# Preparing a sequence in another order: projections, row transfers and the norm reciprocal ahead of the pair loop

## What is computed

```
xp, z  = x @ Wx.T, x @ Wz.T
Bm, Cm = rmsnorm(x @ WB.T) * w + bias, rmsnorm(x @ WC.T) * w + bias   # 64 heads x 128
dt, lam, theta = softplus(x @ Wdt.T), sigmoid(x @ Wlam.T), x @ Wth.T
Bm, Cm = rope(Bm, cumsum(theta * dt)), rope(Cm, cumsum(theta * dt))
h_t = alpha_t h_(t-1) + beta_t B_(t-1) x_(t-1) + gamma_t B_t x_t ;  y_t = C_t h_t
out = (y * silu(z)) @ Wout.T
```

## Time and profile before

| what | value |
|---|---|
| median of 3 runs | 3788.26 us (3786.51 to 3813.47) |
| the profiled execution | 3786.05 us, of which the span of the trace is 3784.2 us |
| mean granted TensorE clock | 0.904 of 2.4 GHz |
| busy share | PE 88%, DVE 76%, ACT 47%, POOL 46% |
| reciprocal L1105 of pairs 0 and 1, sequences 0 to 3 | at 631.3, 1340.1, 2045.6, 2687.5 us |
| first `F_dve1`, sequences 0 to 3 | at 645.0, 1349.5, 2055.9, 2697.3 us |

### The profile page before, as it was taken

One profiled execution on the slowest core, in us unless ns is written; L12 is line 12 of the kernel. 1 busy time (PEld: TensorE's weight loads), 2 busy tenths in 40 slices (PEclk: granted clock), 3 DMA queues, 4 the chain that ended last, 5 costly groups with the idle time before them and its releaser, 6 DMA issues.

```text
span 3784.2 us, 84141 instructions
## 1 busy us (share of the span) xinstructions
PE 3313.2 (88%) x26980; PEld 2650.1 (70%) x26980; DVE 2880.4 (76%) x4774; ACT 1790.7 (47%) x3552; POOL 1733.4 (46%) x1420
## 2 busy tenths in 40 slices
PE   5299986899998889999867999998899998799990
PEld 4288874777776667777755788775577876688880
DVE  5265654999999489999845999994799999465663
ACT  1144434556564256555415666651566665144440
POOL 3433321555555145666501666662366665132326
PEclk7699998999998799999868999997999999699995
DMA  9898974564644154555204555541455453388883
GB/s 389 292 301 278 292 229 141 156 191 153 195 151 136 49 171 142 163 152 160 83 8 128 166 156 162 162 120 55 138 162 150 154 164 111 143 283 295 282 283 120
DMA packets 343082, 668.79 MB, mean 177 GB/s; under 512 B 62272, under 2 KB 183232, under 8 KB 341824
## 3 DMA queue, kind: packets, MB, share of 16 engines
q1 hardware_dynamic: 318272, 598.73, 49.6%
q0 software_dynamic: 24576, 67.14, 6.0%
HBM read 484.03 MB, written 180.62 MB: 176 GB/s over the span
## 4 chain that ended last, share of the span: by engine, by line
PE 57%; DVE 16%; issue 9%; DMA 7%; SPq 6%; ACT 2%; POOL 1%; DVEq 1%; POOLq 0%; ACTq 0%
PE bank L59 14%; PE bank L496 9%; PE bank L509 6%; PE bank L1245 5%; PE bank L1206 4%; PE bank L1275 4%; DVE xbc L1134 3%; SPq L738 3%; PE bank L487 3%; PE bank L1076 3%; DVE tmp L1158 2%; PE bank L1214 2%; PE bank L1266 2%; DMA rr_bc<-rr_dram 2%; DVE xc L1140 2%
## 5 line engine op out<-in xcount | busy, mean ns | idle before, releaser
L59 PE MATMUL bank<-xh,wb 128*128 128x512 f32 x2048 | 717.7, 432 | 36.9 <-DVE sqs L1095 25.0
L1084 ACT ACTIVATE xbc<-bank,norm_w 128x512 f32<-128x512 f32 x512 | 350.0, 684 | 610.5 <-PE bank L59 539.2
L1166 POOL TENSOR_TENSOR rot<-rot,tmp 128x512 f32<-128x512 f32 x256 | 332.2, 1297 | 608.0 <-DVE tmp L1158 608.0
L1158 DVE SCALAR_TENSOR_TENSOR tmp<-xbc,bias,cs_sn 128x1024 f32<-128x1024 f32 x256 | 450.2, 1758 | 0.0
L59 PEld LDWEIGHTS bank<-xh,wb 128*128 128x128 f32 x2048 | 364.0, 196 | 113.6 <-DVE sqs L1095 32.3
L1167 POOL TENSOR_TENSOR rot<-rot,tmp 128x512 f32<-128x512 f32 x256 | 440.9, 1722 | 0.0
L496 PE MATMUL bank<-wgu,xgT 128*128 x2048 | 424.2, 330 | 0.3
L59 PE MATMUL bank<-xl,wb 128*128 128x512 f32 x1024 | 419.5, 410 | 0.0
L556 DVE TENSOR_TENSOR hh<-sg,bank 128x96 f32<-128x96 f32 x512 | 130.2, 254 | 328.9 <-ACT sg L547 326.0
L1158 DVE SCALAR_TENSOR_TENSOR rot<-xbc,bias,cs_sn 128x1024 f32<-128x1024 f32 x256 | 377.0, 1473 | 0.1
L538 ACT ACTIVATE xgT<-bank 128x256 f32<-128x256 f32 x512 | 196.7, 384 | 377.3 <-PE bank L487 375.8
(11 more groups left out here) (210 smaller groups left out, 6735.0 us busy)
## 6 DMA issues: line engine op xcount, KB each, us to landing
wb<-watt_dram SPq DMA_DIRECT2D x96, 1024.0 KB, 6.4
yd<-ys SPq DMA_DIRECT2D x128, 512.0 KB, 4.4
rr_bc<-rr_dram SPq DMA_DIRECT2D x128, 512.0 KB, 6.4
wd<-w_down SPq DMA_DIRECT2D x512, 96.0 KB
xd<-xg SPq DMA_DIRECT2D x16, 2048.0 KB, 23.9
watt_dram<-wb SPq DMA_DIRECT2D x32, 1024.0 KB, 5.6
dt_bc<-row_dram SPq DMA_DIRECT2D x256, 128.0 KB, 5.4
al_bc<-row_dram SPq DMA_DIRECT2D x256, 128.0 KB, 2.9
```

What stands on the lines that cost most here:

```text
L59: ins = e.matmul(dst, a, m, start=start and c == 0, stop=stop and c == n - 1, skip_group_check=not (start and stop))
L1084: e.activation(xbc[j % 4][:, i, :], XBANK[i % 2][:, :], ACT.Copy, scale=norm_w[:, i:i + 1])
L1158: ins = e.scalar_tensor_tensor(o[:, 2 * ty:2 * ty + 2, :], X[:, i, :].unsqueeze(1).to_broadcast([P, 2, SEQ]), bias_of(i), cs_sn[j % 2][:, ...
L1166: e.tensor_tensor(R[:, 2 * ty, :], R[:, 2 * ty, :], tmp[:, 2 * ty + 1, :], ALU.subtract)
```

## The change

On PE the A parts 0 and 1 of pair 1 come directly after pair 0, then ss of pair 0, the other two parts, `inner(0)`, the `dect` transposes, ss of pair 1, `inner(1)`, and then `T_pe` of pair 0, which so far stood in `pairs_pe` behind `x1`; `inner(2)`, `inner(3)` and A of pair 2 come last. On ACT `R_act` moves into the preparation, ahead of the copy to `decay_t`, and A of pair 2 is cut in two and stands behind `T_act2` and `T_act3` of pair 0. On DVE the first `A_dve` of pair 1 moves ahead of the wait for alpha, the reciprocal `R_dve` into the middle of the `x1` products, and `A_dve` of pair 2 behind `T_dve2`. On SP `R_sp` is cut into three: its first DMA, the reciprocal's operand, is issued before the wait for the row stores, the other two between the broadcasts. The splits of sequence 0's weights for pairs 2 and 3 move along.

```diff
@@ -782,21 +782,25 @@
                                        start=k == 0, stop=k == KD - 1)
             ins.then_inc(e_p1.sem, 1)
             e.wait_ge(e_xl.sem, e_xl.at(KD * (b + 1)))
-            A_pe(e, b * NP, 0, None if is_first(b) else (b - 1) * (NP // 2) + 1)
+            first = None if is_first(b) else (b - 1) * (NP // 2) + 1
+            A_pe(e, b * NP, 0, first)
+            A_pe(e, b * NP + 1, 1, first, [0, 1])
+            ss_pe(e, b * NP, 0)
+            A_pe(e, b * NP + 1, 1, first, [2, 3])
             inner(0)
-            inner(1)
-            ss_pe(e, b * NP, 0)
-            A_pe(e, b * NP + 1, 1, None if is_first(b) else (b - 1) * (NP // 2) + 1)
-            e.wait_ge(e_pd.sem, e_pd.at(b * PREP_STEPS + 3))
-            inner(2)
-            inner(3)
-            ss_pe(e, b * NP + 1, 1)
             e.wait_ge(e_p4.sem, e_p4.at(b + 1))
             e.nop(nofuse=True)
             for k in range(NC):
                 ins = e.matmul(W[2][CL:P, k * CL:(k + 1) * CL], dect[:, k * CL:(k + 1) * CL], ident[0:NH, 0:NH],
                                start=True, stop=True)
             ins.then_inc(e_p5.sem, 1)
+            ss_pe(e, b * NP + 1, 1)
+            inner(1)
+            e.wait_ge(e_pd.sem, e_pd.at(b * PREP_STEPS + 3))
+            e.wait_ge(e_p3.sem, e_p3.at(2 * b + 2))
+            T_pe(e, b * NP, 0, first)
+            inner(2)
+            inner(3)
             A_pe(e, b * NP + 2, 2, None if is_first(b) else (b - 1) * (NP // 2) + 2)
 
         def prep_act(e, b):
@@ -829,9 +833,12 @@
             e.activation(alpha, dth, ACT.Exp, scale=neg_a[:, 0:1]).then_inc(e_pc.sem, 1)
             A_act(e, b * NP + 1, 1, [0, 1])
             A_act(e, b * NP + 1, 1, [2, 3])
+            R_act(e, b * (NP // 2))
             e.wait_ge(e_p5.sem, e_p5.at(b + 1))
             src = W[2][CL:P, :].rearrange("p (k a q) -> p k q a", k=NC, a=2)
             e.activation(decay_t[CL:P, :, :, :], src, ACT.Copy).then_inc(e_p3.sem, 1)
+            if is_first(b):
+                wb_high_act(e, 2, 0, 1)
 
         PREP_STEPS = 12
         e_pd, e_pu, e_p6 = ev("e_pd"), ev("e_pu"), ev("e_p6")
@@ -872,6 +879,7 @@
                 ins = e.scalar_tensor_tensor(dtk[:, s], steps_of(s), 0.0, tok(sp_l, s + 1), ALU.max, ALU.add)
             step(ins)
             A_dve(e, b * NP, [1])
+            A_dve(e, b * NP + 1, [0])
             e.wait_ge(e_pc.sem, e_pc.at(6 * b + 6))
             step(e.tensor_copy(alpha0, alpha))
             step(e.memset(starts(alpha0), 0.0))
@@ -883,7 +891,6 @@
             e.memset(end_rows[:, :, 0:1], 0.0)
             ends = dect.rearrange("p (k c) -> p k c", k=NC)[:, 0:NC - 1, CL - 1]
             e.tensor_copy(end_rows[:, :, 1:NC], ends.unsqueeze(1).to_broadcast([NH, 32, NC - 1])).then_inc(e_p4.sem, 1)
-            A_dve(e, b * NP + 1, [0])
             A_dve(e, b * NP + 1, [1])
             e.tensor_tensor(gam, lamk[:, 0], dtk[:, 0], ALU.mult)
             step(e.tensor_scalar(oml, lamk[:, 1], -1.0, 1.0, ALU.mult, ALU.add))
@@ -895,6 +902,10 @@
             assert n[0] == PREP_STEPS
             wide = lambda a, t: a[:, t, :].unsqueeze(2).to_broadcast([P, NH, HP])
             for t in range(TT):
+                if t == 2 and is_first(b):
+                    wb_low_dve(e, 2, 0)
+                if t == 2:
+                    R_dve(e, b * (NP // 2))
                 e.wait_ge(e_p2.sem, e_p2.at(TT * b + t + 1))
                 src = xbanks[t][:, :].rearrange("p (n d) -> p n d", n=NH)
                 ins = e.tensor_tensor(x1[:, :, t, :], src, wide(coef, t), ALU.mult)
@@ -996,12 +1007,17 @@
                     dst = row_dram[:, kp, SEQ + a * (SEQ // 2):SEQ + (a + 1) * (SEQ // 2)]
                     s4 = hrow[r, SEQ:2 * SEQ].rearrange("p (t k c) -> p t k c", t=TT, k=2)
                     e.dma_start(dst.rearrange("q (t c) -> q t c", t=TT), s4[:, :, kp, :]).then_inc(a_roww.sem, 16)
+            R_sp1(e, b * (NP // 2))
             e.wait_ge(a_roww.sem, a_roww.at(8 * (b + 1)))
             e.nop(nofuse=True)
-            for m in range(2):
-                dt_sp(e, m, m)
-                al_sp(e, m, m)
-                end_sp(e, m, m)
+            dt_sp(e, 0, 0)
+            al_sp(e, 0, 0)
+            R_sp2(e, b * (NP // 2), 0)
+            dt_sp(e, 1, 1)
+            R_sp3(e, b * (NP // 2), 0)
+            end_sp(e, 0, 0)
+            al_sp(e, 1, 1)
+            end_sp(e, 1, 1)
 
         def row_sp(e, dst, q, cols, sem):
             for a in range(2):
@@ -1106,15 +1122,19 @@
 
         e_rc = ev("e_rc")
 
-        def R_sp(e, gm, par, cnt):
+        def R_sp1(e, gm):
             e.wait_ge(e_sr.sem, e_sr.at(gm + 1))
             e.nop(nofuse=True)
             e.wait_ge(e_rc.sem, e_rc.at(gm))
             e.nop(nofuse=True)
             e.dma_start(rc_in[:, :], stdr.rearrange("r (c w) -> r c w", w=32)).then_inc(a_r1.sem, 16)
+
+        def R_sp2(e, gm, par):
             e.wait_ge(e_rc.sem, e_rc.at(gm + 1))
             e.nop(nofuse=True)
             e.dma_start(rr_dram[par].rearrange("r (c w) -> (r c) w", w=32), rc[:, :]).then_inc(a_r2.sem, 16)
+
+        def R_sp3(e, gm, par):
             e.wait_ge(a_r2.sem, a_r2.at(gm + 1))
             e.nop(nofuse=True)
             e.wait_ge(e_xcc.sem, e_xcc.at(2 * (gm - 1)))
@@ -1122,6 +1142,11 @@
             for a in range(2):
                 src = rr_dram[par].rearrange("(g a) t -> a g t", a=2)[a:a + 1]
                 e.dma_start(rr_bc[par][CL * a:CL * a + CL, :, :], src.to_broadcast([CL, 4, SEQ])).then_inc(a_rr[par].sem, 16)
+
+        def R_sp(e, gm, par):
+            R_sp1(e, gm)
+            R_sp2(e, gm, par)
+            R_sp3(e, gm, par)
 
         def F_dve1(e, n, j, cnt):
             e.wait_ge(e_X.sem, e_X.at(4 * (n + 1)))
@@ -1457,14 +1482,12 @@
                     e.nop(nofuse=True)
                     al_sp(e, q + 2, j + 2)
                 if RG:
-                    R_sp(e, gm + 1, (j // 2 + 1) % 2, b * NB + it + 1)
+                    R_sp(e, gm + 1, (j // 2 + 1) % 2)
 
         def pairs_pe(e, b):
             N, NB, G = b * NP, NP // UN, b * (NP // 2)
-            e.wait_ge(e_p3.sem, e_p3.at(2 * b + 2))
             e.wait_ge(e_x12.sem, e_x12.at(b + 1))
             e.wait_ge(e_z0.sem, e_z0.at(b + 1))
-            T_pe(e, N, 0, None if is_first(b) else (b - 1) * (NP // 2) + 1)
             turn_pe(e, b, 0, True, False)
             with e.Fori(1, NB - 1) as it:
                 turn_pe(e, b, it, False, False)
@@ -1481,18 +1504,15 @@
 
         def pairs_act(e, b):
             N, NB, G = b * NP, NP // UN, b * (NP // 2)
-            R_act(e, G)
-            if is_first(b):
-                wb_high_act(e, 2, 0, 1)
-            A_act(e, N + 2, 2)
-            if is_first(b):
-                wb_high_act(e, 3, 1, 1)
-            e.wait_ge(e_x12.sem, e_x12.at(b + 1))
-            XP_act(e, N, 0, 0)
             T_act2(e, N, 0)
+            A_act(e, N + 2, 2, [0, 1])
             T_act3(e, N, 0)
             if is_first(b):
                 th_high_act(e, 2, 0, 1)
+                wb_high_act(e, 3, 1, 1)
+            A_act(e, N + 2, 2, [2, 3])
+            e.wait_ge(e_x12.sem, e_x12.at(b + 1))
+            XP_act(e, N, 0, 0)
             turn_act(e, b, 0, True, False)
             with e.Fori(1, NB - 1) as it:
                 turn_act(e, b, it, False, False)
@@ -1516,16 +1536,13 @@
 
         def pairs_dve(e, b):
             N, NB, G = b * NP, NP // UN, b * (NP // 2)
-            if is_first(b):
-                wb_low_dve(e, 2, 0)
-            A_dve(e, N + 2, [0])
-            if is_first(b):
-                wb_low_dve(e, 3, 1)
-            R_dve(e, G)
             T_dve1(e, N, 0, G + 1)
             T_dve2(e, N, 0)
             if is_first(b):
                 th_low_dve(e, 2, 0)
+            A_dve(e, N + 2, [0])
+            if is_first(b):
+                wb_low_dve(e, 3, 1)
             turn_dve(e, b, 0, True, False)
             with e.Fori(1, NB - 1) as it:
                 turn_dve(e, b, it, False, False)
@@ -1537,7 +1554,6 @@
 
         def pairs_sp(e, b):
             N, NB, G = b * NP, NP // UN, b * (NP // 2)
-            R_sp(e, G, 0, b * NB + 1)
             e.wait_ge(e_th.sem, e_th.at(N + 1))
             e.nop(nofuse=True)
             th_load_sp(e, b, 2, 0)
```

## The result

| what | before | changed |
|---|---|---|
| median | 3793.2 us (4 runs) | 3757.2 us (4 runs, 3751.97 to 3768.14) |
| ratio of the two | | 0.990, 95% interval 0.9855 to 0.9945 |
| profiled execution, its span | 3786.05, 3784.2 us | 3757.49, 3755.7 us |
| busy us of PE, DVE, ACT, POOL | 3313.2, 2880.4, 1790.7, 1733.4 | 3298.7, 2877.2, 1790.6, 1731.0 |

The change is faster: in this first measurement by 1%, 36 us between the medians (interval 21 to 55), where 13 were forecast.

A forecast was written before the change was run, and what follows sets the result against it. Two chains of nearly equal length were taken to end at each sequence's first product with `rr_bc` (L1134). Gains 1.9 + 2.9 + 2.4 + 5.0 = 12.2 from 3786.05 gave 3773.8 to 3776.0, said as 3775, range 3759 to 3787.

The forecast's parts named there:

- the walk of sequence 1: Unit-by-unit count of PE, ACT, DVE and SP times up to the first product with `rr_bc`: gain 1.9 us.
- theta's raw weights: Sequence 0, pair 2: issued by SP after all broadcasts at 624.4, taken as 5.6, there at 630.0; sequence gain 5.0.
- theta's size: PE's theta product counted as twelve matmuls, 2.8 us; theta of pair 1, behind pair 2, was to end last.
- case at full clock: Sequence 1 with PE at full clock: ACT's side would be last, a gain of 3.3 instead of 1.9.
- The clock term: PE stands 2.3 in pair 2, then runs at 1.2 GHz: part 2 ends at 1339.8, theta of pair 1 at 1345.5.
- The table load: ACT's load for the root, 1.28, was taken as done while idle; behind the wait it costs +0.9 a chain, 4 in all.
- The head start passes in full: Rival: angle and fraction 7.1 earlier move each first product by that, 28 in all, 3759; chance 0.13.
- Slower by the detour: Rival: pair 2's A parts 2 and 3 and pair 1's theta hang on dt(0)'s arrival; 3791 with the median; chance 0.08.
- The same time: Rival: finish line moves, but first turns wait again for a later transfer or POOL, eating the lead: 3787; chance 0.11.
- The operand does not do what it says: Rival: `R_dve` waits amid `x1` longer than the queue gained; 8.7 idle in sequence 0, covered if operand lands before about 618.
- signs of being wrong: L1134 of sequence 1 moved over 4 or later; `dt_bc` wait above 1 us; second DMA wait; difference in loops or experts.
- signs of being right: `rc_in` before broadcasts; angle some 7 earlier; `rr_bc` landed early; DVE idle on PE's theta or ACT's squares; clock near 0.5.

The follow-up runs named there:

- again: The changed kernel once more, unchanged, with more rounds, against the kernel before: ratio 0.9946 (0.9924 to 0.9968), 21 us by the ratio.
- again2: The changed kernel once more, unchanged, on another chip, against the kernel before: ratio 0.9926 (0.9894 to 0.9958), 28 us.
- a2_around: From the changed kernel: ACT does pair 2's parts 0 and 1 before pair 0's angle, 2 and 3 before its absolute value; ratios to before 0.9912 and 0.9903.
- sp_only: From the kernel before: only SP's queue in the changed order, PE, ACT and DVE as before; ratio 0.9968 (0.9951 to 0.9985), 12 us.
- pair1_late: From the changed kernel: pair 1's projections and first DVE add back in their old places; ratio to the kernel before 0.9987 (0.997 to 1.0004).

## Why the prediction was wrong

**What held.** The path was the right one up to the last chain, and the walk of sequence 1 held to 0.9 us up to the last square. As offsets, counted and then measured: pair 1's last matmul 26.4, 26.7; first row store 28.1, 27.9; `decay_t` copied 32.3, 32.9; reciprocal 34.2, 34.5; angle of pair 0 40.3, 39.4; square of part 1 of pair 2 45.1, 44.4; last square 50.4, 49.6. ACT's list was counted at 8 with no hole and took 8.2. In sequence 0 the reciprocal was counted to hold DVE for 8.7 under cover and held it for 8.59, and theta's raw weights were last, as the rows show (DVE, sequence 0, start 564.30; against the earlier trace rows):

```profile
611.63 0.35 DVE L1121 RECIPROCAL rc<-rc_in 128x32 f32<-128x32 f32 x1 [8.59 <-DMA rc_in<-decay_t]
...
615.53 0.70 DVE L1049 SCALAR_TENSOR_TENSOR bank<-bank,dt_bc 128x512 f32<-128x512 f32 x1 [1.83 <-DMA dt_bc<-row_dram]
...
627.12 0.42 DVE L971 TENSOR_TENSOR th<-th_raw,th 128x256 fp32r<-128x256 f32 x1 [8.18 <-ACT th L967]
...
635.59 2.33 DVE L1159 TENSOR_TENSOR xbc<-xbc,rr_bc 128x1024 f32<-128x1024 f32 x2
```

**The step that failed: theta's size.** "the theta product (twelve matmuls, 2.8)". It has six: the PE rows above go from 1310.96 to `inner(2)` at 1312.46, 1.5. The trace of the kernel before had it too, with theta of pair 1 as six matmuls from 1344.05 to 1346.74, 2.7 at the lower clock:

```profile
1344.05 1.19 PE L59 MATMUL bank<-xh,th 128*128 128x512 f32 x2 [6.12 <-DVE nfr L1042]
1345.04 0.63 PE L59 MATMUL bank<-xl,th 128*128 128x512 f32 x1
1345.46 1.06 PE L59 MATMUL bank<-xh,th 128*128 128x512 f32 x2
1346.32 0.63 PE L59 MATMUL bank<-xl,th 128*128 128x512 f32 x1
1346.74 1.06 PE L59 MATMUL bank<-xh,wb 128*128 128x512 f32 x2
```

I had taken the two parts of the weight split and the two halves of the contraction for four times three. This enters twice. Ahead of `inner(2)` it makes the angle 0.9 earlier than counted. And behind pair 2 it had put PE last: theta of pair 1 was to end at offset 52.4, and ended at 48.2, 1.4 before ACT's last square. So the wrong size also named the wrong last wait for sequences 1 to 3: it was ACT's list, which the prediction had only as its case at full clock.

**The clock term went with it.** I took 1.2 GHz behind the gap PE makes in pair 2, and charged 1.4 us a sequence. The gap came nearly as counted (2.3), 2.46 in sequence 1 (PE rows above) and 2.47 in sequences 2 and 3. Its effect did not: in sequence 1 the next pair of matmuls took 0.73, full clock, in sequence 2 it took 1.22, the lower level. The two PE rows of sequence 2:

```profile
2009.26 0.71 PE L59 MATMUL bank<-xh,th 128*128 128x512 f32 x2 [1.24 <-ACT decay_t L839]
...
2019.60 1.22 PE L59 MATMUL bank<-xh,wb 128*128 128x512 f32 x2 [2.47 <-ACT sqt L1103]
```

Yet from the angle to the product it took 12.7 in sequence 1 and 12.8 in 2 and 3: with six matmuls PE's theta is through before ACT's last square even where the lower clock came, in sequence 2 at 2025.5 against 2025.8. The Trainium skill (TensorE: Matmul & The Clock Gate, section "Why this matters for your kernels") advises against idle gaps of PE between bursts of matmuls, and means longer ones than this. The trace shows that the lower clock can follow here too, in two sequences of three, and that it costs nothing where PE is not last. In sequence 0 PE is last: theta of pair 1 took 2.6 at the lower clock, and DVE waited 0.66 for it.

**The sum with the right size.** With six matmuls and nothing else changed, the angle of sequence 1 starts 0.9 earlier, theta of pair 1, at half of the 3.1 counted for twelve, ends at 1343.1, and ACT's side, now last, comes 0.9 earlier than the 1344.2 + 1.95 of the prediction, to 1345.25: a gain of 4.2 where 1.9 was forecast and 4.3 measured. (With all six at the lower clock, 2.7 as in the rows above, it would be 3.3.) The same 2.3 more make 5.2 and 4.7 in sequences 2 and 3 (5.6 and 4.3 measured). In sequence 0 theta of pair 1 took 2.6 where I had 3.7, and the raw weights 4.7 from issue to use where I had 5.6: 7.0 instead of 5.0 (7.1 measured). Together 21.1, against 21.3 measured. So the forecast of 12.2 was short by 9, some 8 of it through the miscounted product and 0.9 through the raw weights.

In sequences 2 and 3 the agreement is partly luck. Their row stores moved by 4.5 and 3.8 us, where those of sequence 1 moved by 2.9 (from offsets 32.1, 31.8 and 30.8 to 27.6, 28.0 and 27.9), and the table load below took about as much back; the sum counts neither.

With 21 instead of 12 the forecast would have been 3766, inside the range. The other 9 us down to 3757.2 are not the mechanism's; they are taken up under "The rest of the 36 us".

**The table load.** I kept 1.3 in the range for a load behind the wait. It depends on the sequence. In the written-out sequence 1 ACT loads at 1306.05 and then waits 2.23 for the sums (rows above); in the loop body of sequences 2 and 3 it waits first:

```profile
2006.41 1.28 ACT L1116 ACT_TABLE_LOAD   x1 [3.60 <-PE bank L1092]
```

There theta of pair 0 waits 1.24 for `decay_t` (PE, 2009.26), and the angle starts at 40.3 and 40.9 instead of 39.4. From the first row store to the angle it took 12.7 and 12.9 there, against 11.5 in sequence 1; again and again2 show the same difference, 1.1 to 1.6.

**The rivals.** *The head start passes in full* (28 us, 3759): by the first total the nearest, by mechanism wrong. The angle came 8.0 earlier in sequence 1, and the first product 4.3: ACT's list took the rest, as a2_around shows by giving 3.7 of it back. a2_around itself comes near this rival, with 34 and 37 us. *Slower by the detour*: dt(0) was waited for only in sequence 0, 1.83. *The same time*: the changed kernel keeps its lead, sp_only 12 us of 19.5. *The operand does not do what it says*: true in a milder form, it does nothing. Of the prediction's own signs of being wrong two came: L1134 of sequence 1 moved by 4.3, over 4, and sequence 0 waited 1.83 for `dt_bc`, over 1. Of its signs of being right, the clock near 0.5 did not come in sequence 1, where the 3.3 us behind the gap have 1.00; in sequence 2 the 3.4 us behind it have 0.53. Its seven broadcasts behind `rr_bc` are six in the rows of SP, which changes nothing in the sum.

**The rest of the 36 us.** The first measurement is of four runs a side. The median before was 3788.26 when the forecast was made and 3793.2 with a fourth run, so 5 of the 36 lie on that side. Of the 28.5 between the two spans, 2.3 lie ahead of the first preparation, 21.3 in the offsets, 4.9 in the loops and the last expert phase. The stretch ahead of the first preparation holds no changed instruction; it took 566.6 and 576.9 in two executions before, 564.3, 578.7 and 568.5 after. The one from the fourth first product to the end took 1086.9 and 1093.0 before, 1089.2, 1088.0 and 1077.3 after. So single executions differ by 10 us and more in code that is the same, and a median of four carries it. The 4.9 did not come again either: all that lies outside the four offsets took 3532.7 and 3545.3 before, 3525.5, 3549.7 and 3546.5 after, on average 3539 and 3541. The three intervals of the changed kernel overlap from 0.9924 to 0.9945, 21 to 29 us, with the head start of 23 inside. So nothing here points to a gain in the loops; one of some 5 us is below what five profiles can tell, and it stays open.

## What to carry to other kernels

Find the instruction at which the steady loop starts and count every chain that ends there; when one is shortened, the next one's length decides, here ACT's, with two projections that had been moved behind the angle and its table load. Count matmuls of a helper in the trace, not in the code. A single wait or DMA that is moved earlier is worth nothing if the instruction behind it waits for something else, and parts of a reordering may only pay together: SP's order alone gave 19.5 of 23 us of head start, the whole change without pair 1's new place gave 9.

## What was not expected of the hardware

The same gap of PE, 2.46 to 2.47 us, was followed by 2.4 GHz in sequence 1 (the next pair of matmuls took 0.73) and by 1.2 GHz in sequences 2 and 3 (1.20 to 1.22), in all three profiles of the changed kernel. In pair1_late a gap of 2.46 to 2.51 was followed by 0.73 in all three sequences. So the length of the gap alone does not tell which level follows; no run here shows what does. And ACT's table load of 1.28 us stood ahead of a wait in the written-out code and behind the same wait in the loop body, in the same three profiles, and there theta of pair 0 waited 1.24 us for it.
